# Two 64-row tiles for the TensorE transposes of an attention and ternary FFN kernel

## The reference, cut to what matters

```python
q = heads(layernorm(x), Wq, bq); k = heads(ctx, Wk, bk); v = heads(ctx, Wv, bv)
q_prime = relu(einsum('bhnd,fd->bhnf', q, Wqf))
k_prime = relu(einsum('bhnd,fd->bhnf', k, Wkf)) * mask
kv  = einsum('bhnf,bhne->bhfe', k_prime, v)
out = einsum('bhmf,bhfe->bhme', q_prime, kv) / (einsum('bhmf,bhf->bhm', q_prime, k_sum) + 1e-8)
x = x + out @ Wo.T + bo
# FFN: quantize rows of layernorm(x) to 8 bits, ternary gate/up
a = up * relu(gate)**2;  a = rmsnorm(a) * g
x = x + quantized(a) @ ternary(w_down).T
```

## Time and profile before

| what | us |
|---|---|
| median of three runs | 454.1 |
| profiled execution, its device time | 454.95 |
| span of the profiled execution | 453.2 |
| PE busy | 439.6 |
| PEld (weight loads, overlapping PE) busy | 342.4 |
| DVE busy | 367.0 |
| ACT busy | 298.0 |
| POOL busy | 130.7 |

### The profile page before, as it was taken

The page is one execution under the profiler, slowest core; times in us unless marked ns, Lnnn a source line. Parts: engine busy times, 40 slices in busy tenths (PEclk is TensorE's granted clock), DMA queues, the critical chain, the costliest instruction groups (busy, mean ns, idle before and its releaser), DMA issues.

```text
span 453.2 us, 10053 instructions
## 1 busy us (share of the span) xinstructions
PE 439.6 (97%) x4147; PEld 342.4 (76%) x4147; DVE 367.0 (81%) x635; ACT 298.0 (66%) x426; POOL 130.7 (29%) x280
## 2 busy tenths in 40 slices
PE   8999899999999999999999999999999999899995
PEld 5888889888999878958767776796877777684443
DVE  4735929358966989999989999898999898898992
ACT  5766969764232276786686768578575975738982
POOL 0000000005420644342342541444235054224430
PEclk9999999999999999999999999999999999999999
DMA  7991917423400210251223225025122123233045
GB/s 237 417 381 48 346 77 244 175 88 106 184 3 24 94 25 0 48 128 37 48 71 69 54 44 115 23 48 128 37 46 57 39 46 58 72 82 58 14 106 149
DMA packets 53085, 45.61 MB, mean 101 GB/s; under 512 B 43440, under 2 KB 44336, under 8 KB 51120
## 3 DMA queue, kind: packets, MB, share of 16 engines
q1 hardware_dynamic: 53040, 44.98, 34.1%
HBM read 27.14 MB, written 4.19 MB: 69 GB/s over the span
## 4 chain that ended last, share of the span: by engine, by line
PE 71%; DVE 13%; ACT 8%; issue 3%; DMA 2%; POOL 1%; SPq 0%; DVEq 0%; ACTq 0%
PE ps L344 63%; ACT rb L347 4%; PE ps L581 3%; DVE zb L350 3%; PE ps L558 3%; DVE tk L788 2%; PE ps L612 2%; ACT rbe L347 2%; ACT zb L347 1%; DMA xs<-in_wk_dram 1%; DVE qol L350 1%; DVE yqb L815 1%; ACT aph L347 1%; DMA yqTq<-yqb 1%; DMA xqT<-xqb 1%
## 5 line engine op out<-in xcount | busy, mean ns | idle before, releaser
L344 PE MATMUL ps<-tg,xqT 128*128 128x512 bf16 x256 | 68.1, 386 | 1.0 <-DMA xqT<-xqb 1.0
L344 PE MATMUL ps<-tu,xqT 128*128 128x512 bf16 x256 | 68.2, 385 | 0.0
L344 PE MATMUL ps<-td,yqT 128*128 128x512 bf16 x208 | 50.7, 385 | 0.0
L347 ACT ACTIVATE rb<-zb 128x1024 f32<-128x1024 f32 x29 | 30.6, 1055 | 28.8 <-DVE zb L350 28.8
L353 POOL TENSOR_SCALAR tk<-tk 128x1 f32<-128x1 f32 x96 | 37.4, 390 | 41.2 <-DVE tk L739 21.3
L347 ACT ACTIVATE zb<-zb,cm,tk 128x1024 f32<-128x1024 f32 x29 | 34.8, 1235 | 14.8 <-POOL tk L350 14.8
L347 ACT ACTIVATE rb<-ps 128x1024 f32<-128x1024 f32 x29 | 29.6, 1020 | 19.0 <-PE ps L344 18.1
L344 PEld LDWEIGHTS ps<-tu,xqT 128*128 128x128 bf16 x256 | 25.1, 98 | 21.5
L344 PE MATMUL ps<-kvh,apl 128*128 128x66 f32 x112 | 41.1, 367 | 0.0
L344 PE MATMUL ps<-kvh,aph 128*128 128x66 f32 x112 | 40.3, 359 | 0.3 <-DVE apl L356 0.3
L344 PE MATMUL ps<-kvl,aph 128*128 128x66 f32 x112 | 40.4, 361 | 0.0
(11 more groups left out here) (149 smaller groups left out, 1262.3 us busy)
## 6 DMA issues: line engine op xcount, KB each, us to landing
xs<-in_wg_dram SPq DMA_DIRECT2D x4, 1024.0 KB, 13.3
xs<-in_wu_dram SPq DMA_DIRECT2D x4, 1024.0 KB, 6.7
xs<-in_wd_dram SPq DMA_DIRECT2D x4, 1024.0 KB, 8.0
xs<-in_x_dram SPq DMA_DIRECT2D x8, 512.0 KB, 5.6
out_dram<-xs SPq DMA_DIRECT2D x15, 256.0 KB, 2.2
craw<-in_ctx_dram SPq DMA_DIRECT2D x7, 512.0 KB, 7.2
qoh<-qol SPq DMA_DIRECT2D x12, 128.0 KB, 2.2
qy<-qol SPq DMA_DIRECT2D x12, 128.0 KB, 2.4
```

Of the source, the lines that this page charges most:

```text
L344: return add("pe", name, cost, waits, lambda e: e.matmul(out, lhsT, rhs, start=start, stop=stop))
L347: return add("act", name, cost, waits, lambda e: e.activation(out, in_, func, **kw))
```

## The change

`transposes` does each transpose of 128 x 128 as two, one for rows 0 to 63 and one for rows 64 to 127 of the source, each in its own 64-row tile of the array (`tile_position`), against a 64 x 64 identity. The two write to two neighbouring banks, 64 columns for each of the four blocks, so that a row tile fills 256 columns of both. `pair_of_banks` hands the two out: from `listed`, or from the round of 4 to 7, where it skips one bank if the next would be 5 or 7. ACT and DVE read both banks in one instruction with the same number of elements as before. Both banks are then free when `.lo` is done. The lists of banks in the program text are lengthened, and the planner's costs are 0.055 for each of the 8 in place of 0.109 for each of 4.

```diff
-           "oT#.#": 0.109, "xT#.#": 0.109},
+           "oT#.#.#": 0.055, "xT#.#.#": 0.055},
@@ ln1
-                war = [f"oT{i - 2}.3"] if a else [f"warm{WARM - 1}"]
+                war = [f"oT{i - 2}.3.0", f"oT{i - 2}.3.1"] if a else [f"warm{WARM - 1}"]
@@
+        def pair_of_banks():
+
+            if listed:
+                return listed.pop(0), listed.pop(0)
+            turn[0] += turn[0] % 2
+            return bank(), bank()
+
         def transposes(tag, t, waits):
-            b = bank()
+
+            b, b2 = pair_of_banks()
+            assert b2 == b + 1
+            ends = []
             for kc in range(KC):
-                out, src = ps[:, b, P * kc:P * kc + P], xn[:, t, P * kc:P * kc + P]
-                add("pe", f"{tag}.{kc}", 0.11, (waits + bank_user[b] + ["small"]) if kc == 0 else [], lambda e, out=out, src=src: e.transpose(out, src, eye))
-            return b, f"{tag}.3"
+                for r in range(2):
+                    rows = slice(64 * r, 64 * r + 64)
+                    out, src, one = ps[:, b + r, 64 * kc:64 * kc + 64], xn[rows, t, P * kc:P * kc + P], eye[rows, rows]
+                    k = add("pe", f"{tag}.{kc}.{r}", 0.055, (waits + bank_user[b + r] + ["small"]) if kc == 0 else [],
+                            lambda e, out=out, src=src, one=one, at=(64 * r, 0): e.transpose(out, src, one, tile_position=at))
+                    if kc == KC - 1:
+                        ends.append(k)
+            return b, ends, ps[:, b:b + 2, 0:256].rearrange("p r (a c) -> p r a c", a=KC)
@@ s1
+            b, ends, src = transposes(f"xT{i}", t, [f"xn{i}"])
+                return z[:, 0:1024].rearrange("p (a t r c) -> p t r a c", a=KC, t=2, r=2)[:, t]
+            act(f"xT{i}.hi", 0.5, ends, cols(aph), src, ACT.Copy)
+            bank_user[b] = bank_user[b + 1] = [tt("dve", f"xT{i}.lo", 0.62, ends + [f"xT{i}.hi"], cols(apl), src, f32(cols(aph)), ALU.subtract)]
@@ s5: the same for oT, qoh and qol
@@ batch 0 and 1
-                listed += [4, 5]
+                listed += [4, 5, 0, 1]
-        listed += [4, 5, 6, 7, 4, 5, 6, 7]
+        listed += [4, 5, 0, 1, 6, 4, 5, 0, 1, 7, 2, 3]
```

More of the change, by code:

```diff
@@ L615, in s1 @@
+            return b, ends, ps[:, b:b + 2, 0:256].rearrange("p r (a c) -> p r a c", a=KC)
         def s1(a, t):
             i = 2 * a + t
-            b, k = transposes(f"xT{i}", t, [f"xn{i}"])
-            src = ps[:, b, :].rearrange("p (a c) -> p a c", a=KC)
+            b, ends, src = transposes(f"xT{i}", t, [f"xn{i}"])
             def cols(z):
-                return z[:, 0:1024].rearrange("p (a c) -> p a c", a=KC)[:, :, P * t:P * t + P]
-            act(f"xT{i}.hi", 0.5, [k], cols(aph), src, ACT.Copy)
@@ L623, in s1 @@
-            bank_user[b] = [tt("dve", f"xT{i}.lo", 0.62, [k, f"xT{i}.hi"], cols(apl), src, f32(cols(aph)), ALU.subtract)]
+                return z[:, 0:1024].rearrange("p (a t r c) -> p t r a c", a=KC, t=2, r=2)[:, t]
+            act(f"xT{i}.hi", 0.5, ends, cols(aph), src, ACT.Copy)
+            bank_user[b] = bank_user[b + 1] = [tt("dve", f"xT{i}.lo", 0.62, ends + [f"xT{i}.hi"], cols(apl), src, f32(cols(aph)), ALU.subtract)]
         def s2(a, halves=range(2)):
@@ L718, in s5, with cols @@
             tt("pool", f"xbo{i}", 1.23, [f"xn{i}", "bo"], xs[:, i, :], xs[:, i, :], bo_b[:, :], ALU.add)
[L719 to L722, removed]
+            b, ends, src = transposes(f"oT{i}", t, [f"on{i}.0", f"on{i}.1"])
+            def cols(z):
+                return z[:, 512 * t:512 * t + 512].rearrange("p (a r c) -> p r a c", a=KC, r=2)
+            act(f"oT{i}.hi", 0.5, ends, cols(qoh), src, ACT.Copy)
+            bank_user[b] = bank_user[b + 1] = [tt("dve", f"oT{i}.lo", 0.62, ends + [f"oT{i}.hi"], cols(qol), src, f32(cols(qoh)), ALU.subtract)]
         def col(k, i):
```

## The result

The changed kernel is slower: 472.96 us (median of 4 runs, 471.23 to 475.25) against 454.17 us (4 runs), a ratio of 1.0418, 95% interval 1.0392 to 1.0443. The forecast was 467.6 us, with a range of 459 to 475. The profiled execution took 474.21 us, with a span of 472.4 us; that of the kernel before took 454.95 us.

The account below looks back on a forecast made before the run. PE was taken to bound the main loop, with DVE at 93%. Bank waits and turns of 10.2 + 1.3 + 1.4 + 1.2 + 1.4 = 15.5, less 2 given back, put 13.5 on 454.95: median 467.6 us, range 459 to 475.

Parts of the forecast that it names:

- the six places: In passes p = 0 to 5, s6(a,1) waits for .lo: 1.7 us each (floor 1.27), +10.2 us; s1(n,1) waits for x1.
- the small waits: New PE waits for banks outside the six-pass sequence: xT1 +1.3, at3.1 and at13.1 +1.4, tail +1.2 us.
- xT1 behind features(6): xT1 writes banks 0 and 1, just filled by features(6), and waits for two DVE steps: +1.3 us.
- at3.1 and at13.1: In p = 0 and 5 they get the bank of at3.0 and at13.0: 0.7 us each, +1.4 us.
- D10 and pr14: In the tail D10 gets at15.0's bank and pr14 gets D10's: 0 to 3 us, taken as +1.2.
- 14 single row tiles, turns less gain: oT2 to oT15: each gains 0.20 us and pays 0.30 for turns, +0.10 each, +1.4 us in all.
- given back: PE delays absorbed where PE waits in the tail and DVE has caught up: -2 us.
- The transposes: Two tiles side by side, 0.06 us a pair: a row tile takes 0.24 us, a gain of 0.20.
- The turns: Going in and out of the tiled form costs 0.30 us for a group, between 0 and 0.39; 23 groups.
- Not slower: Rival: DVE sets the pace, so only shorter transposes (-6.4 us) and turns (+3) count: 451 us; chance 0.08.
- The change doesn't do what it says: Rival: the two tiles don't overlap, 473 us, or load slowly, 482 us; chance 0.11.
- Only the floors: Rival: 1.27 us lost per pass, other waits at low ends, 3 to 5 us given back: 459.5 us; chance 0.13.

Follow-up runs that it names:

- run 1: The kernel before with its full-array transposes, but each row tile holds a pair of banks as in the changed kernel: 469.84 us, ratio 1.0333.
- run 5: Changed kernel with tiles, other banks listed so the new waits vanish, PE order kept except xT1 behind keys(7): 456.69 us, ratio 1.0059.
- run 9: Changed kernel with other banks only at the end of each of the six passes; the other waits stay: 461.75 us, ratio 1.0173.
- run 4: Changed kernel with the two loops in transposes exchanged, rows 0 to 63 first: a single execution of 469.72 us.
- run 11: Run 5's kernel with only the .lo wait before s6(a,1) put back, six times: 466.58 us, ratio 1.0276.
- run 7: The changed kernel again without edit, on the chip of the other runs: 471.06 us, ratio 1.0379.
- Run 6: Run 5's banks and order with full-array transposes in place of the 64-row tiles: 454.94 us, ratio 1.0028.
- run 10: Run 5's kernel with only the x1 wait before s1(n,1) put back, six times: 464.70 us, ratio 1.023.
- run 8: Changed kernel with the two loops in transposes exchanged, as in run 4, this time timed: 471.04 us, ratio 1.0391.
- run 2: Changed kernel with tiles, banks relisted and PE steps moved to cover the waits, the down projection before s2: 477.26 us, ratio 1.0495.
- run 3: Run 2's order and pairs of banks with full-array transposes: 474.62 us, ratio 1.0459.

## Why the prediction was right, point by point

The mechanism held: run 1 has the loss without the tiles, run 5 has the tiles without the loss. The sum came close in part by luck, since its terms err both ways: the six places were put too high and the small waits too low. These are the terms, as forecast and as the two profiled executions (454.95 and 474.21 us, 19.3 us apart) and the runs show them; the small waits are PE's idle times, and the last row is what remains of the 19.3 us:

| term | forecast, us | measured, us |
|---|---|---|
| the six places (x1 and .lo) | +10.2 | +8.5 (run 9: 8.4) |
| xT1 behind features(6) | +1.3 | +2.1 |
| at3.1 and at13.1 | +1.4 | +2.7 |
| D10 and pr14 | +1.2 | +2.0 |
| 14 single row tiles, turns less gain | +1.4 | +1.5 |
| lowered clock | 0 | +3.3 in the profiled execution, 0 to 5 |
| given back, and all else | -2 | -0.8 (remainder) |

- **The transposes.** Right. The load in a 64-row tile lasts 138 ns, a pair of tiles steps by 0.06 us, and the two tiles run side by side (run 4). The step behind the first pair of a group is 0.11 us, so that 8 transposes take 0.24 us from first to last start.
- **The turns.** Right in sum. Between two matmuls of 512 columns a single row tile went from 0.67 us (288.76 to 289.43) to 0.72 (297.10 to 297.82); before s6 it went from 0.57 to 0.70. With what the next steps add (0.01 and 0.02) the loss is 0.06 and 0.15 us, in the mean 0.11 against the 0.10 forecast. That PE drains at the turn, as the Trainium skill says (TensorEngine Tiling (Array Packing), section Tiling Modes), agrees with the 0.32 us before a group against 0.22 to 0.23 before. Here are rows of both kernels at such a place, first the kernel before:

```profile
288.76 0.40 PE L344 MATMUL ps<-tu,xqT 128*128 128x512 bf16 x1
288.99 0.60 PE L612 MATMUL ps<-small,xn 128*128 128x128 f32 x4
289.43 0.38 PE L344 MATMUL ps<-tu,xqT 128*128 128x512 bf16 x1
```

The changed kernel:

```profile
297.10 0.40 PE L344 MATMUL ps<-tu,xqT 128*128 128x512 bf16 x1
297.43 0.46 PE L625 MATMUL ps<-small,xn 64*128 64x64 f32 x8
297.82 0.39 PE L344 MATMUL ps<-tu,xqT 128*128 128x512 bf16 x1
```

- **The six places.** The floor of 1.27 us was close (1.30 to 1.44 in the middle passes, 1.47 and 1.58 in the first and last). The 0.4 us for steps that DVE or ACT would take up in between were too much: at the place shown DVE had none there. The forecast left the wait for x1 out of its sum, which cost it little, as run 11 has nearly the whole loss from the `.lo` wait alone (1.33 us).
- **The small waits were put too low**, all three for one reason: I let DVE's steps come forward to, or near, the first moment at which they could run. They did not. The steps into `kp` ran at 114.72 us, where they had been, behind two steps of `td`; on3.0 waited for a reduction of 1.22 us; at D10, on15.0 ran behind a step of 1.22 us into `zb`. In this execution the better guess was the DVE times of before, unchanged. xT1's wait is not a fixed one: in the second profile of the changed kernel (run 7) PE came 0.7 us earlier and the steps into `kp` began 1.3 us earlier, at 113.38 us, and the wait cost 1.5 us, near the 1.3 forecast.

```profile
113.50 1.30 DVE L470 TENSOR_SCALAR td<-td 128x2048 bf16<-128x2048 bf16 x2
114.72 1.27 DVE L356 SCALAR_TENSOR_TENSOR kp<-ps,small 128x512 f32<-128x512 f32 x2
177.96 1.22 DVE L804 TENSOR_REDUCE tk<-zb 128x1 f32<-128x1024 f32 x1
179.52 0.42 DVE L350 TENSOR_TENSOR xn<-ps,rd 128x256 f32<-128x256 f32 x1
```

- **What was given back.** At the first matmul of s6(6, 1) the changed kernel is 15.0 us behind the kernel before (387.72 against 372.72 us), and at the last one before oT14 it is 13.5 us behind (411.73 against 398.27 us). So the tail gives back 1.5 us, near the 2 forecast; small differences elsewhere take 0.7 of it, and their cause is not shown.
- **The clock was missing.** The 5.4 us between forecast and median are the small waits (2.9 too low in sum), less 1.7 at the six places, 1.2 not given back, and the lowered clock, some 3 us at the median.
- **The rivals.** "Not slower" needed waits under 0.5 us a pass; PE loses 1.4. Its own sum was also off: with the turns at the 0.30 us that the prediction takes elsewhere, 23 groups cost 6.9 us and not 3, which makes it about no change. "The change doesn't do what it says" is out by the 0.24 us for a row tile and by run 4. "Only the floors" had the six places nearly right (7.6 us) but relied on 4 us given back.

No version tried beats the kernel before. Run 6 (454.94 us) holds pairs of banks without using them, and is 0.3% above it; its tiled twin, run 5, is above that. A pair of row tiles gains 0.04 us and a single one loses 0.107, so with every wait covered the tiles still cost about 14 x 0.107 - 9 x 0.04 = 1.1 us.

## What to carry to other kernels

A change that takes a second PSUM bank for a step must be priced by who used that bank last and what work lies in between, before anything is said of the array: write out the order of the banks and look for pairs where the reader has only just been given its data. Where PE was full here, a matmul group of 2.7 us between the two writers of a bank covered a copy and a subtraction (0.57 and 0.69 us) at every place but one (0.42 us left in run 10); another group of transposes (0.4 us) did not. And a step moved as cover uncovers whatever it had been hiding.

## What the runs showed of the hardware

- PE starts the transposes of a second 64-row tile beside the first's though four others stand ahead of them in the program: in run 8 the fourth and the eighth of the text start seventh and eighth, at 217.77 and 217.78 us (and likewise at every row tile of that trace but xT1, whose second half waited for its bank).
- The granted clock fell to half, for 3.4 or 6.8 us at a time, each time during or shortly behind an idle time of PE of 1.47 to 3.15 us. In the changed kernel it is 414.8 to 421.6 us, behind the wait of 1.56 us at D10. In run 7's profile it is 376.5 to 379.9, behind a wait of 1.47 us at at13.1, and 414.1 to 420.9. In run 2's it is 205.3 to 212.1 and 249.7 to 253.1, at waits of 2.87 and 1.98 us. In run 10's it is 188.3 to 191.7 and 382.9 to 386.3, at waits of 1.99 and 1.54 us, and in run 11's 382.7 to 386.1, at the wait of 3.15 us.
- Runs 5 and 6, which have no such idle times in that part, stayed at 1.000 in all of their 17 executions. The kernel before stayed there in 34 of the 37 executions beside the runs; of the others two had 0.999 and one 0.996. What decides is not settled: run 1, with a wait of 1.39 us at D10, stayed at 0.999 or 1.000 in five of five, run 8, with 1.55 us, fell in two of four, and run 3's profiled execution stayed at 1.000 with waits of up to 2.7 us.
